# Masked 16-head attention over four experts: PSUM banks regrouped from 3 + 3 to 2 pairs + 2, with one VectorE maximum over two heads

## The reference, cut to what matters

```python
q = (xg @ wq[e] + bq[e]).reshape(b, s, h, hd)      # h = 16 heads, hd = 8
att = jnp.einsum('bqhd,bkhd->bhqk', q, k) * sm_scale
att = jnp.where(validg[:, None, None, :], att, -1000000000.0)
att = jax.nn.softmax(att, axis=-1)                 # rows of 256 keys
y = jnp.einsum('bhqk,bkhd->bqhd', att, v).reshape(b, s, d)
y = y @ wo[e] + bo[e]
out = out.at[bidx, order].add(wg[..., None] * y)
```

## Time and profile before

| what | us |
|---|---|
| runs before, median of 3 | 2358.84 (2354.91 to 2360.76) |
| span of the profiled execution | 2356.1 |
| busy: TensorE | 2100.5 (89%) |
| busy: VectorE | 1806.2 (77%) |
| busy: ScalarE | 1460.9 (62%) |
| busy: GpSimd | 693.0 (29%) |
| a1, roughly 580 to 820 of the span | 240 |
| a2, roughly 1100 to 2190 of the span | 1090 |

### The profile page before, as it was taken

One profiled execution on the slowest core, in us unless ns is written; L12 is line 12 of the kernel. 1 busy time (PEld: TensorE's weight loads), 2 busy tenths in 40 slices (PEclk: granted clock), 3 DMA queues, 4 the chain that ended last, 5 costly groups with the idle time before them and its releaser, 6 DMA issues. The chain is left out here.

```text
span 2356.1 us, 66550 instructions
## 1 busy us (share of the span) xinstructions
PE 2100.5 (89%) x21573; PEld 1247.3 (53%) x21573; DVE 1806.2 (77%) x4556; ACT 1460.9 (62%) x3730; POOL 693.0 (29%) x1221
## 2 busy tenths in 40 slices
PE   5999999986899896666899999999999988888798
PEld 4777777754455453443445555555555544444355
DVE  7878887745788645775789999999999878776563
ACT  3655565532488723322678888888888877777431
POOL 2111111101344000222343344344433455552110
PEclk9999999998699997776799999999999999999899
DMA  5000000001343000001334434443444333331000
GB/s 162 2 2 2 2 2 2 2 1 36 120 129 123 30 1 1 1 0 53 126 123 127 131 127 128 128 133 126 129 130 131 124 107 105 103 100 56 1 18 19
DMA packets 198397, 167.47 MB, mean 71 GB/s; under 512 B 15445, under 2 KB 178198, under 8 KB 198198
## 3 DMA queue, kind: packets, MB, share of 16 engines
q1 hardware_dynamic: 198198, 164.90, 22.1%
HBM read 85.42 MB, written 77.63 MB: 69 GB/s over the span
## 5 line engine op out<-in xcount | busy, mean ns | idle before, releaser
L831 DVE TENSOR_REDUCE a_rowmax<-a_psS 128x2 f32<-128x512 f32 x1536 | 965.2, 684 | 141.3 <-PE a_psS L596 137.2
L754 ACT ACTIVATE a_probs<-a_psT 128x512 f32<-128x512 f32 x1536 | 830.6, 601 | 228.5 <-PE a_psT L603 228.1
L596 PE MATMUL a_psS<-stackk,stackq 49*128 49x256 bf16 x3072 | 498.8, 279 | 45.2 <-DMA stackq<-a_negmaxT 14.7
L603 PE MATMUL a_psT<-stackq,stackk 51*128 51x256 bf16 x3072 | 482.4, 274 | 2.1 <-ACT a_probs L754 1.9
L645 PE MATMUL a_psO<-a_probs,values 128*32 128x256 f32 x6144 | 413.9, 387 | 1.4 <-ACT a_probs L754 1.4
L596 PEld LDWEIGHTS a_psS<-stackk,stackq 49*128 49x128 bf16 x3072 | 220.8, 95 | 295.2 <-DVE a_rowmax L831 113.8
L645 PEld LDWEIGHTS a_psO<-a_probs,values 128*32 128x32 f32 x6144 | 161.0, 109 | 146.4 <-issue 51.3
L1175 ACT ACTIVATE a_probs<-a_psS,a_negmax 128x256 f32<-128x256 f32 x256 | 121.0, 473 | 183.0 <-DVE a_negmax L1199 183.0
L603 PEld LDWEIGHTS a_psT<-stackq,stackk 51*128 51x128 bf16 x3072 | 217.5, 94 | 19.2 <-ACT a_probs L754 8.1
L1059 POOL TENSOR_TENSOR a_vr<-a_v,a_rsum 128x256 f32<-128x256 f32 x128 | 79.8, 623 | 392.1 <-DVE a_rsum L1260 371.8
L1197 DVE CUSTOM_DVE_ANT_0 a_psS<-a_psS,causal 128x256 f32<-128x256 f32 x256 | 114.8, 448 | 72.1 <-PE a_psS L1081 60.2
(11 more groups left out here) (305 smaller groups left out, 3907.1 us busy)
## 6 DMA issues: line engine op xcount, KB each, us to landing
a_scratch<-a_parts SPq DMA_DIRECT2D x192, 192.0 KB, 2.4
stackq<-a_scratch SPq DMA_DIRECT2D x192, 192.0 KB
stackk<-a_scratch SPq DMA_DIRECT2D x192, 192.0 KB
a_scratch<-a_parts SPq DMA_DIRECT2D x192, 128.0 KB, 2.3
a_scratch<-a_parts SPq DMA_DIRECT2D x192, 64.0 KB, 1.9
stackq<-a_negmaxT SPq DMA_DIRECT2D x192, 8.0 KB
x<-in_x SPq DMA_DIRECT2D x4, 512.0 KB, 6.2
out<-x SPq DMA_DIRECT2D x8, 256.0 KB, 2.3
```

The costliest lines, as they stand in the source:

```text
L596: return pe.matmul(psS[score_bank(s, u)[0]][:, t * SEQ:(t + 1) * SEQ], stackq[r:r + MAX_ROW, b, pr, t * P:(t + 1) * P], stackk[r:r + MAX_R ...
L603: return pe.matmul(psT[shifted_bank(s, u)[0]][:, t * SEQ:(t + 1) * SEQ], stackk[r:r + ZERO_ROW, b, pr, t * P:(t + 1) * P], stackq[r:r + ZE ...
L754: act.activation(probs[:, h, :], psT[shifted_bank(s, u)[0]][:, :], ACT.Exp, scale=of(s, off).exp_scale).then_inc(exp_done, 1)
L831: dve.tensor_reduce(rowmax[:, s.parity(1), u, :], psS[score_bank(s, u)[0]][:, :].rearrange("p (t k) -> p t k", t=2), AX_X, ALU.max).then_i ...
```

## The change

Scores get four banks in place of three, as two pairs of two. The heads u and u+1 (u even) share a pair; TensorE waits for a free pair at even slots only, until the maximum of the pair before the last has been taken. VectorE waits for both heads and takes the maxima of both in one instruction, 8 to a job in place of 16. Shifted scores get two banks in place of three: `ring` now gives a distance of two slots. The semaphore `max_done` counts pairs, and GpSimd waits for 8 of them in place of 16. The router, which borrows banks ahead of the loop, gets the halves of the first pair and the first half of the second.

```diff
-SCORE_BANKS, SHIFTED_BANKS, MISC_BANKS = 3, 3, 1
+SCORE_PAIRS, SHIFTED_BANKS, MISC_BANKS = 2, 2, 1
+HEAD_PAIRS = HEADS // 2
...
-        psS = [ctx.enter_context(nc.psum_tensor(f"{name}_psS{k}", [P, 512], F32)) for k in range(SCORE_BANKS)]
+        psS = [ctx.enter_context(nc.psum_tensor(f"{name}_psS{k}", [P, 2, 512], F32)) for k in range(SCORE_PAIRS)]
...
-        def score_bank(s, u):
+        def score_bank(u):
-            return score_ring[s.quarter(0) * HEADS + u]
+            return psS[u // 2 % SCORE_PAIRS][:, u % 2, :]
...
-                    back = score_bank(s, u)[1]
-                    if s.known(1, 1) or u >= back:
-                        pe.wait_ge(max_done, s.n(1, HEADS, u + 1 - back))
+                    if u % 2 == 0 and (s.known(1, 1) or u >= 2 * SCORE_PAIRS):
+                        pe.wait_ge(max_done, s.n(1, HEAD_PAIRS, u // 2 + 1 - SCORE_PAIRS))
...
-                dve.wait_ge(scores_ready, s.n(1, HEADS, u + 1))
+                dve.wait_ge(scores_ready, s.n(1, HEADS, u + 2))
...
-                dve.tensor_reduce(rowmax[:, s.parity(1), u, :], psS[score_bank(s, u)[0]][:, :].rearrange("p (t k) -> p t k", t=2),
+                dve.tensor_reduce(rowmax[:, s.parity(1), u:u + 2, :].rearrange("p h t -> p (h t)"),
+                                  psS[u // 2 % SCORE_PAIRS][:, :, :].rearrange("p h (t k) -> p (h t) k", t=2),
                                   AX_X, ALU.max).then_inc(max_done, 1)
...
-                    if s.has(1):
+                    if s.has(1) and u % 2 == 0:
                         maxima(s, u)
...
-                wait_alone(pool, max_done, s.n(0, HEADS, HEADS), pool_passed)
+                wait_alone(pool, max_done, s.n(0, HEAD_PAIRS, HEAD_PAIRS), pool_passed)
```

More of the change, by code:

```diff
@@ L449, in attention8 @@
         shared = [ctx.enter_context(nc.psum_tensor(f"{name}_shared{k}", [P, 512], F32)) for k in range(MISC_BANKS)]
-        score_ring, shifted_ring = ring(SCORE_BANKS, unroll * HEADS), ring(SHIFTED_BANKS, unroll * HEADS)
+        shifted_ring = ring(SHIFTED_BANKS, unroll * HEADS)
         norm = Norm(m, sem, sb, psT[0:2])
-        route = Router(m, w, sem, sb, norm, psS[0:2], psS[2], probs) if masked else None
+        route = Router(m, w, sem, sb, norm, [psS[0][:, 0, :], psS[0][:, 1, :]], psS[1][:, 0, :], probs) if masked else None
         scratch = nc.dram_tensor(f"{name}_scratch", (2, 2, 6, P, SEQ), BF16, kind="Internal").ap()
@@ L595, in scores_part @@
                 r, b = GROUP_ROWS * i, s.quarter(1)
-                return pe.matmul(psS[score_bank(s, u)[0]][:, t * SEQ:(t + 1) * SEQ], stackq[r:r + MAX_ROW, b, pr, t * P:(t + 1) * P],
+                return pe.matmul(score_bank(u)[:, t * SEQ:(t + 1) * SEQ], stackq[r:r + MAX_ROW, b, pr, t * P:(t + 1) * P],
                                  stackk[r:r + MAX_ROW, b, pr, :], start=True, stop=True, tile_position=(r, 0))
```

## The result

The changed kernel takes 2677.9 us (median of 4 runs, 2675.6 to 2682.2) against 2358.1 us before in the same comparison; the ratio is 1.135, with a 95% interval of 1.133 to 1.137. The forecast was 2580 us, with a range of 2470 to 2670. The sign and the main mechanism came as forecast, the size did not: 320 us were lost where 221 were expected.

What follows compares the result with a forecast made beforehand. The prediction took TensorE as the bound, with next to no slack. Waits for shifted-score banks, 2.72 us a clean step and 2.43 a mean expert step, summed to 221 us over all stretches: 2359 + 221 = 2580 us, range 2470 to 2670.

Steps and rivals of the forecast that it cites:

- What bounds the kernel: Clean expert step: TensorE busy 12.07 of 12.20 us, writing heads in bursts; VectorE and ScalarE catch up during its other work.
- Banks of shifted scores: TensorE's slots 3, 6, 9, 13 wait for ScalarE's exponentials two back: 2.72 us a step, bounds 2.55 and 2.85.
- Banks of scores: TensorE's even slots wait for the pair two back: cost nothing; if margins go, 0.1 to 0.3 us a step.
- Maxima of two heads: VectorE's pair maximum takes 1.10 us (bounds 1.07 to 1.20), saving 0.8 us a step, entered as nothing on the path.
- The fourth rival: TensorE's clock falls to 0.85 as its busy share drops: step about 17 us, 2763 us; chance 10%.
- its milder form: TensorE's clock falls in a part of the steps alone: 2650 to 2700 us.
- Late steps: The late steps' four waits, 2.65 us in all, partly hidden under existing waits: 2.4 us each, bounds 1.6 and 2.7.
- Sum: Added waits over expert, late and a1 steps, first a2 steps and edges: together 221 us.
- The lower bound of 185 us: Sum with 2.55 us in clean steps, DMA waits not hidden and not grown, 1.6 us in late steps: about 185.
- VectorE sets the step: VectorE's saved time frees TensorE down to 12.07 us a step: faster, 2321 us; chance 4%.
- only the number of banks counts: Eight PSUM banks in use before and after, so no change: 2359 us; chance 3%.
- Half of it: ScalarE gets ahead at slots 9 and 13, or TensorE has hidden slack: 1.3 us a step, 2477 us; chance 12%.

Runs made afterwards that it cites:

- Experiment 1: Kernel before the change with two banks of shifted scores in place of three, nothing else changed: 2619.3 us, ratio 1.109.
- experiment 3: Changed kernel with VectorE's `add_output` ahead of the maximum of heads 10 and 11 in place of behind it: 2592.1 us, ratio 1.099.
- experiment 8: Changed kernel with both `add_output` and `normalise` of VectorE ahead of the pair's maximum, TensorE's order unchanged: 2596.5 us, ratio 1.101.
- Experiment 9: Kernel before with four single score banks, two shifted-score banks, one maximum a head, and `prob_values` 0, `project_out`, `project_v` each one slot earlier: 2459.2 us, ratio 1.043.
- spread order: TensorE's `prob_values` 0, `project_out` and `project_v` after slots 2, 8, 12, not 3, 9, 13; on the changed kernel with `add_output` first: 2503.8 us.
- experiment 2: Kernel before with four single banks of scores and two of shifted scores, one maximum a head: 2627.1 us, ratio 1.111.
- experiment 5: Experiment 4's kernel with VectorE's `normalise` ahead of the maximum of heads 2 and 3: 2567.6 us, ratio 1.087.
- experiment 4: Experiment 3's kernel with TensorE's `prob_values` 0, `project_out` and `project_v` after slots 2, 8, 12 in place of 3, 9, 13: 2503.8 us, ratio 1.061.

## Why the prediction was wrong in size and right in its main mechanism

**What bounds the kernel** held. TensorE had no slack, the two readers caught up in its pauses, and the banks were what let it run ahead.

**Banks of shifted scores.** Right, slot by slot: 0.83, 0.43, 0.68 and 0.67 us were measured for 0.84, 0.46, 0.71 and 0.71. The sum of 2.72 us came to 2.61; the way back from ScalarE to TensorE was 0.05 us (the exponential at 1617.28 lasts 0.60, the slot it held began at 1617.93), nearer the one row seen than the 0.08 taken. Experiment 1 shows this term by itself. The waits for the DMA of the maxima went under as forecast (TensorE's matmuls: 14.7 us in 18 places before, 2.7 in 2 after).

**Banks of scores: "Cost nothing".** This is the step that failed. The forecast asked for each slot of TensorE whether the pair's maximum was done in time. That was right: no slot waited for one in the clean step. It did not ask the same of what is queued behind the pair's maximum on VectorE. A pair's maximum of slot 10 waits for slot 11, `add_output` behind it waits too, and it holds the one shared bank that `project_v` needs. The run with `add_output` ahead of the maximum is 86 us faster (experiment 3); the wait itself, 0.79 us in the clean step, makes 74 us of that if it is the same in all 94 steps. The same holds for `normalise` behind the pair of slot 2, 0.19 us at `turn_max`, but that one went under slot 6's wait (experiment 8). Experiment 9 has the same mechanism in the spread order: where slot 6 doesn't cover it, the pairs cost 45 us.

**Maxima of two heads.** Two in a row took 2.36 us:

```profile
1617.24 2.36 DVE L831 TENSOR_REDUCE a_rowmax<-a_psS 128x4 f32<-128x1024 f32 x2 [0.93 <-PE a_psS L597]
```

That is 2.36 - 1.22 = 1.14 us each in a row, inside the bounds (1.07 to 1.20) and near the 1.10 taken. As forecast it went to idle time. The Trainium skill's figure (Perfetto Trace Analysis, Optimizing Scalar/DVE Operations) would give 0.125 us saved a pair; the rows give 1.20 - 1.14 = 0.06, and it is the rows that hold for this kernel. But the coarser instruction is not worth nothing here: with `add_output` out of its way (experiment 3) the pairs are 35 us faster than four singles (experiment 2), 14.79 for a mean of 15.0 us a step. Whether that is VectorE's time or the single wait of every second slot (experiment 1) stays open.

**The clock.** The fourth rival put 10% on 0.85 throughout. It was wrong in the expert stretch as a whole, 0.98, but right that new waits would cost some clock: about 17 us. The forecast's sum held no term for it. The measured 2678 us lies in the band of its milder form, 2650 to 2700, and this is chance: most of what brought the time there is `project_v`. The view of one window (0.87 us of wait at clock 1.00) could not show what two waits close together do.

**Late steps.** 3.5 us each were measured (63.0 / 18) for 2.4. Experiment 3 still has 2.7 (322.7 - 273.3 = 49.4 us over 18), so 0.8 is `project_v` again. Some of these steps last 19 to 20 us in the kernels with two banks in the old order (the changed one and experiments 1, 2, 3 and 8), where the others last 17.8 to 18.4, and the clock of the late stretch is 0.95 to 0.96; how much of it is a cause and how much goes with the late steps' own long waits stays open.

**Sum.** 221 forecast, less 10 for the shorter way back, 74 for `project_v`, some 17 for the clock in the expert stretch: 302. The other 18 us are spread over the steps of a2, the late ones and the edges, and are not settled. With `add_output` out of the way the forecast's sum is nearly met: experiment 3 lost 236 us of span (2592.1 against 2356.1). The lower bound of 185 us in the forecast doesn't follow from the conditions given with it: with the DMA waits not hidden, 2.55 us more in each of 56 steps are 143 and the sum is over 200; near 190 comes out when those waits are hidden.

**The rivals on the other side.** *VectorE sets the step* and *only the number of banks counts* are out by experiments 1 and 2: all eight banks are in use in the second too, and it loses 266 us. *Half of it* is out by the table: none of the four waits came smaller by more than 0.04 us. By the rule that all 8 PSUM banks be used (the Trainium skill, Perfetto Trace Analysis, Matmul Optimizations) the two splits stand equal, and the times, 2361 and 2627 us, do not bear that out: one bank moved from the reader that needed three to one that had enough.

## What to carry to other kernels

Count banks against the longest run of writes between two pauses of the writer, for each reader by itself: here a run of three writes on two banks waited for the rest of the round trip, 0.7 us, and a run of two for 0.2 to 0.4 us or not at all (moving the bank cost 266 us in one order and 13 in the other). When an instruction is made coarser and starts later, look not only at who waits for its result but at everything queued behind it on its engine, and at what those hold; moving `add_output` ahead of it was worth 86 us. A wait that was cheap because other work stood beside it is not cheap once that work is moved.

## What the runs showed of the hardware

In the expert stretch of these kernels the falls of TensorE's clock went with waits that stand close together, and not with the sum of the waits. The changed kernel waits 0.78 and then 1.00 us with one slot between and shows dips; experiment 5 has 0.95 and 0.87 with `turn_max` and one slot between, and shows them too (0.97 from 1200 to 1900 us). The longest wait of experiment 3 is 1.23 us and that of experiment 4 is 1.41, each with no other long one beside it, and from 1200 to 1900 us the steps of each are within 0.05 us of each other at a granted clock of 1.00. TensorE's busy share doesn't order them: 86% in experiment 3 (599 of 700 us, no dips), 89% in experiment 5 (626 of 700, dips). The waits stand in every step, the dips come in about every eighth of the changed kernel and every third or fourth of experiment 5; what exactly brings one about was not tested.
